# Moving one bias addition of VectorE across two steps of a mixture-of-experts loop

## The reference, cut to what matters

```python
gate = gelu(einsum('besd,edf->besf', slots, Wg) + bg)     # B=4, E=16, S=64, D=256, F=512
up   = einsum('besd,edf->besf', slots, Wu) + bu
eout = einsum('besf,efo->beso', gate * up, Wd) + bd       # bd: one row of 256 for each expert
y    = einsum('bns,bso->bno', combine, eout)
```

## Time and profile before

| | |
|---|---|
| median of 3 runs | 1989.15 us (1987.82 to 1989.57) |
| the profiled execution's own time | 1985.45 us |
| its span in the profile | 1983.4 us |
| TensorE busy | 92% of the span |
| VectorE busy | 68% |
| ScalarE busy | 55% |
| GpSimd busy | 45% |
| TensorE in 538.30 to 649.40 us (12 experts) | 106.72 us busy, 864 matmuls |
| VectorE in the same stretch | 95.52 us busy |
| GpSimd in the same stretch | 76.32 us busy |

### The profile page before, as it was taken

How to read it: one execution, slowest core, us unless ns; L and a number is a source line. 1 busy time by engine, 2 the same in 40 slices (tenths; PEclk the granted TensorE clock), 3 DMA queues, 4 the chain that set the end, 5 groups by cost and what they waited for, 6 DMA issues and landing times. The chain is left out here.

```text
span 1983.4 us, 35336 instructions
## 1 busy us (share of the span) xinstructions
PE 1827.8 (92%) x11720; PEld 1633.2 (82%) x11720; DVE 1340.6 (68%) x2421; ACT 1089.3 (55%) x2146; POOL 895.2 (45%) x1029
## 2 busy tenths in 40 slices
PE   1889999999999899959999968999999999989999
PEld 1778787878899899958999956888878789989998
DVE  5775666554688888835555458666665548888886
ACT  1465556556555677724444325556655655557775
POOL 1454544414666455412222226446443346655553
PEclk9999999999999999979999989999999899999999
DMA  2553334322465577721222145333332426546774
GB/s 65 185 197 126 120 148 148 128 104 99 136 228 173 175 257 264 261 74 54 74 63 63 43 147 213 135 111 149 145 141 107 148 56 216 188 156 234 256 261 164
DMA packets 106670, 298.25 MB, mean 150 GB/s; under 512 B 16256, under 2 KB 56320, under 8 KB 94272
## 3 DMA queue, kind: packets, MB, share of 16 engines
q1 hardware_dynamic: 106560, 296.88, 42.1%
HBM read 187.63 MB, written 109.22 MB: 150 GB/s over the span
## 5 line engine op out<-in xcount | busy, mean ns | idle before, releaser
L115 POOL TENSOR_TENSOR pool_carrier<-minus_half 128x1 f32<-128x1 f32 x236 | 76.3, 323 | 565.4 <-PE f2bank L737 133.0
L596 ACT ACTIVATE f1r_lt<-f1bank,slot_shift 128x512 f32<-128x512 f32 x128 | 88.1, 688 | 171.2 <-PE f1bank L694 171.2
L596 ACT ACTIVATE f2r_lt<-f2bank,slot_shift 128x512 f32<-128x512 f32 x128 | 88.2, 689 | 170.6 <-PE f2bank L694 170.6
L485 DVE TENSOR_TENSOR f1r_e_lo<-f1bank,f1r_e_hi 128x512 fp32r<-128x512 f32 x128 | 82.6, 685 | 91.7 <-ACT f1r_e_hi L659 91.1
L485 DVE TENSOR_TENSOR f2r_e_lo<-f2bank,f2r_e_hi 128x512 fp32r<-128x512 f32 x128 | 82.7, 685 | 91.5 <-ACT f2r_e_hi L659 90.9
L1333 PE MATMUL f2bank<-f2c_eo,f2c_e_hi 128*128 128x258 f32 (+1 forms) x512 | 131.5, 288 | 3.5 <-DVE f2c_eo L1250 3.4
L1333 PE MATMUL f1bank<-f1c_eo,f1c_e_hi 128*128 128x258 f32 (+1 forms) x512 | 130.8, 287 | 3.7 <-DVE f1c_eo L1250 3.4
L1334 PE MATMUL f2bank<-f2c_eo,f2c_e_hi 128*128 128x256 f32 (+1 forms) x512 | 129.6, 284 | 0.0
L1334 PE MATMUL f1bank<-f1c_eo,f1c_e_hi 128*128 128x256 f32 (+1 forms) x512 | 128.9, 283 | 0.0
L1205 POOL TENSOR_TENSOR f2c_e_lo<-f2c_lt,f2c_e_hi 128x512 fp32r<-128x512 f32 x64 | 83.0, 1297 | 91.9 <-ACT f2c_e_hi L1304 91.8
L1205 POOL TENSOR_TENSOR f1c_e_lo<-f1c_lt,f1c_e_hi 128x512 fp32r<-128x512 f32 x64 | 83.1, 1298 | 90.8 <-ACT f1c_e_hi L1304 90.7
(11 more groups left out here) (321 smaller groups left out, 6611.7 us busy)
## 6 DMA issues: line engine op xcount, KB each, us to landing
logits<-f1r_lt SPq DMA_DIRECT2D x16, 2048.0 KB, 7.3
f1c_lt<-logits SPq DMA_DIRECT2D x32, 1024.0 KB, 7.1
logits<-f2r_lt SPq DMA_DIRECT2D x16, 2048.0 KB, 7.3
f2c_lt<-logits SPq DMA_DIRECT2D x32, 1024.0 KB, 7.1
f1r_xin<-in_L_attn_x SPq DMA_DIRECT2D x16, 512.0 KB, 4.8
normalized<-f1r_xin SPq DMA_DIRECT2D x16, 512.0 KB, 2.7
f1r_xback<-normalized SPq DMA_DIRECT2D x16, 512.0 KB, 8.1
f1e_raw_g<-in_L_ffn_Wg SPq DMA_DIRECT2D x16, 512.0 KB, 4.1
```

What stands on the lines that cost most here:

```text
L115: pool.tensor_tensor(c["pool_carrier"][:, col:col + 1], c["minus_half"][:, 0:1], c["minus_half"][:, 0:1], ALU.add)
L485: dve.tensor_tensor(e_lo[t % 2][:, h * BANK:(h + 1) * BANK], ps_t[h][:, :], rd(e_hi[t % 2][:, h * BANK:(h + 1) * BANK]), ALU.subtract).the ...
L596: act.activation(lt[:, g, sc, :], ps_l[sc % 2][:, :], ACT.Identity, bias=c["slot_shift"][:, sc:sc + 1]).then_inc(logit_out, 1)
```

## The change

`rows_out` is taken from behind `h_lo` and put ahead of it, and it handles the rows of expert e-2 instead of e-1. The rows of the last two experts, 14 and 15, both come at the end, behind `combine.first_shifts`. No instruction is added or removed, and its operands are the same.

```diff
                     dve.scalar_tensor_tensor(out=gel[q][:, f, :], in0=ps_h[f][:, R:2 * R],
                                              scalar=c["biases"][:, bass.ds(E * KF + e * KF + f, 1)],
                                              in1=gel[q][:, f, :], op0=ALU.add, op1=ALU.mult).then_inc(hidden_out, 1)
+                if not first:
+                    rows_out(e - 2, pair - 1, q)
                 dve.wait_ge(h_hi_done, e + 1)
                 dve.tensor_tensor(h_lo[q][:, :, :], gel[q][:, :, :], rd(h_hi[q][:, :, :]), ALU.subtract).then_inc(h_lo_done, 1)
-                if not (first and q == 0):
-                    rows_out(e - 1, pair - 1 + q, 1 - q)
 
         emit(0, True, False)
         with dve.Fori(1, E // 2 - 1) as pair:
             emit(pair, False, False)
         emit(E // 2 - 1, False, True)
         combine.first_shifts(dve)
-        rows_out(E - 1, E // 2 - 1, 1)
+        for q in range(2):
+            rows_out(E - 2 + q, E // 2 - 1, q)
```

## The result

The changed kernel takes 1997.68 us (median of 9 runs, 1993.94 to 2002.48); the kernel before takes 1989.57 us beside it. The ratio is 1.0036 with a 95% interval of 1.0022 to 1.0049: it is slower, by 4 to 10 us. The forecast was no change, 1989.9 us, in a range of 1984 to 1995 us; the time lies above the range.

What follows compares the result with a forecast made beforehand. The bound was a chain of GpSimd and VectorE subtractions excluding each other, with TensorE, at 18.53 us a pair. Two mixtures of 0 + 0.2 + 0.15 us added 0.7 to 1989.15, giving 1989.9 us, range 1984 to 1995 us.

Steps and rivals of the forecast that it cites:

- The middle of the stage: Expert loop: filling the gap ahead of `h_lo` comes back as longer durations; gain 0 to 0.12 us a pair, taken as 0.
- The forecast of over 3 us for `lo_g`: Behind `h_lo`: `lo_g` stands still until `lo_u` ends, rising from 1.62 to 3.4 us or more.
- 5.2 + 8.0 us: First expert stage: `hidden` waiting for VectorE's gate-up product, added up to 13.1 us, nearly all the waits listed.
- near 13 us a mixture: Sign in the changed profile: TensorE's wait for line 1006, VectorE's gate-up product, should still be near this size.
- The rival that the gap is real time: Expert stage: VectorE's own chain sets the period, so 16.8 us less, 1972 us; 14%.
- The rival of a late `h_lo`: Middle of the stage: `rows_out` makes `h_lo` 0.7 us later, up to 9.8 us in all, 1999 us; 9%.
- The collision: SyncE's queue: first logits (2 MB) issued just ahead of expert 6's weights, 2 to 4 us late on ScalarE; 0.2 us a mixture.
- part of this is absorbed: Expert 6's lateness: `lo_g` can precede the late `lo_u`, TensorE has 1.25 us a pair to catch up; 0.2 us taken.
- The end of the stage: Handover to combine: line 1250 0.13 us later, ScalarE's queue up to 1.4 us later; 0.15 us taken, 1 us at worst.
- The sum: Whole kernel: two mixtures of 0 + 0.2 + 0.15 us, +0.7 us, forecast 1989.9 us.
- The third rival: Logits ahead of expert 6's weights cost 2 us or more a mixture, handover at worst; +5 to +7 us, 1995 us; 4%.

Runs made afterwards that it cites:

- both: Changed kernel, first logits issued ahead of expert 3's bias load, rows of expert 14 written ahead of the four first shifts; 0.9996 of the kernel before.
- logits early: Changed kernel, SyncE issuing the 2 MB of first logits ahead of expert 3's bias load, not behind it; 1992.87 us, 1.0006 of the kernel before.
- the kernel before with late logits: Kernel before plus one SyncE wait, so the first logits are issued only when `hi_g` of expert 5 is done; 1.0026 of the kernel before.

## Why the prediction was wrong, point by point

*The middle of the stage*: right. The chain `lo_d`, `h_lo`, `lo_u`, `lo_g`, `in_lo` sets the period; "both" shows the reorder to be neutral (0.9996), and halving or moving `lo_u` shows what holds it. The means of `h_lo` and `lo_g` moved as said. The forecast of over 3 us for `lo_g` was too high as a mean, since `lo_g` goes first in part of the pairs; from expert 8 on every one takes 3.42 us in f1.

One reading there was wrong and carried nothing: 5.2 + 8.0 us are the waits of TensorE's matmuls and of its weight loads for the same products, and overlap. Added up they count a stall twice; by the period TensorE loses 7 x 1.25 us, some 9 us, in f1. The sign "near 13 us a mixture" came out as 7.4 + 8.6 = 16.0 us in f1 and 6.2 + 8.6 = 14.8 us in f2, with the stall in it.

*The rival that the gap is real time*, 14%: refuted by "both", whose period stays at 18.5 us with the gap filled. *The rival of a late `h_lo`*, 9%: it has the right sign and the wrong mechanism; it was refuted by "logits early" and "both".

*The collision*: the step that failed. Its mechanism, its place (552.54 us, which is 550.5 us when counted from the first `in_lo` as in the kernel before; forecast 551) and the lateness of 2 to 4 us were as forecast: `hi_g` of expert 6 begins 2.5 us late in f1 and 3.4 us in f2. What failed is "part of this is absorbed", by TensorE's 1.25 us a pair and a swap of `lo_g` and `lo_u`, and with it the 0.2 us that I took from a range of "between nothing and 2 us". TensorE's idle time is no slack: it stands behind a chain of the other engines that has a period of 18.5 us of its own, and once `in_lo` is late, the products, the release of the banks and the next `down` are late too. The odd experts kept their 0.6 us to the end of the stage. The runs show 0.6 and 0.9 us without a fall of the clock, and 2.2 to 2.9 us with one, over the range's end; the clock wasn't in the sum at all.

*The end of the stage*: the second term that was mis-sized. I took 0.15 us for each mixture and gave 1 us as the worst. It was 1.1 and 1.0 us in the change and 0.9 us alone. The lateness of ScalarE's queue was forecast (1.4 us); what I didn't see is that it puts GpSimd's first low part just ahead of line 1251, so the exclusion that I had counted with in the middle struck here.

*The sum*: by the stretches the collision took 0.6 + 2.9 us and the end of the stage 1.1 + 1.0 us, 5.6 us where 0.7 us were forecast. The two terms measured by themselves, 1.0026 and 1.0018, make 0.44%, against 0.36% (7.2 us) of the change, inside their intervals. The third rival, "the collision doesn't get absorbed, with the end of the stage at its worst", 4%, at 1995 us, is nearest to what happened; its 2 us or more in each mixture were reached in f2 alone in the profiled execution.

What stays open: why the clock fell behind the stall in f2 of three kernels and in f1 of one, and not in f1 of two others. It fell behind stalls of 1.83, 1.88, 2.43 and 2.48 us, and not behind 1.74 and 1.82 us; 1.82 and 1.83 us lie too close for the length of the stall to be called the reason. In f1 of the change a fall that the other executions have at the stage's begin (the granted clock of the kernel before is 0.50 in 514 to 516 us) was missing too, so the 0.6 us of that stage may be some 0.2 us too small: from `hidden(0)` to `hidden(2)` it took 15.85 us against 16.05 us in the kernel before. In which of the timed runs the clock fell isn't known, so how much of the 7.2 us is the clock's isn't either.

## What to carry to other kernels

Before filling an engine's gap, look whether its instructions run at their lone duration; where they end at a fixed distance behind another engine's (1.08 us here), the gap is spare time and comes back as standing still. Shorten or move the work that the two engines exclude each other with first: then the same reorder can pay. Idle time of the busiest engine is no cover for a late step either, when it waits for a chain that has no slack of its own. And when a step moves later, follow everything that waits for it through the queue of every engine, down to a DMA queue in which a large, unhurried load then stands ahead of an urgent one.

## What the runs showed of the hardware

TensorE's granted clock: a stall of 2.43 us was followed by over 3 us at the lower level, with matmuls 0.21 to 0.22 us apart instead of 0.12; a stall of 1.82 us in f1 of the same execution was not. In the kernel before with late logits a stall of 1.74 us without a fall cost 0.9 us and one of 1.83 us with a fall cost 2.5 us.

VectorE's subtraction of 128 x 1024 from SBUF took 1.23 us alone, against GpSimd's 2.40 us, and they exclude each other. With `rows_out` out of the line, moving one from GpSimd to VectorE shortened the pair by 1.1 us, though VectorE was the engine with hardly any idle time; with `rows_out` in the line the same move made it 0.7 us longer.

VectorE's additions and products that read PSUM were never held: in all twelve profiles each of the four additions of `rows_out` took 0.40 to 0.43 us and each product of line 1006 took 0.47 to 0.49 us, whatever GpSimd did.
